# A four-layer cross-attention and mixture-of-experts kernel: three slots for the combine weights, three for the raw expert tiles, and several steps placed anew

## The chip, the cores and the metric

The kernel runs on one core of one Trainium2 chip, as one launch. The metric is the device time of that launch in microseconds (us), taken as the median of several runs. The core's engines are TensorE (PE; PEld is its weight load), VectorE (DVE), ScalarE (ACT), GpSimd (POOL) and SyncE (SP); SPq is SyncE's queue, from which most transfers are issued.

## The reference, cut to what matters

Tokens x are 4 x 256 rows of 256 numbers. Four layers follow one another; each adds a gated cross-attention against a context of 4 x 512 rows and then a gated feed-forward:

```python
x = x + tanh(g_xattn[i]) * xattn_i(layernorm(x), ctx)
x = x + tanh(g_ffn[i]) * ffn_i(layernorm(x))
```

Layers 0, 2 and 3 have attention with 16 heads of 16 numbers, layer 1 one with a single head (the "memory" attention). Feed-forwards 0, 1 and 3 are mixtures of experts: a router picks K of E experts per token (2 of 8, 2 of 8, 6 of 16), and a shared expert is added. Cut to its core, one of them is:

```python
probs = softmax(xf @ gate_w.T)
w, idx = top_k(probs, K)
combine = scatter(w, idx)                  # tokens x experts
act = silu(xf @ w_gate[e]) * (xf @ w_up[e])
out = sum_e(combine[:, e] * (act @ w_down[e])) + shared(xf)
```

Feed-forward 2 has no router: it multiplies by the signs of its weights, with 1024 hidden units.

## The kernel before, in words

**Precision.** Matrix operands in full precision are split in a high half (a rounded copy, written by ScalarE) and a low half (the difference, written by VectorE or GpSimd), and a product is the sum of three matmuls: high by high, high by low, low by high (`passes`, whose matmul is L615).

**Tiles of a feed-forward.** The hidden units of all experts stand one after another and are cut in tiles of 128: 14, 10, 8 and 25 tiles for the four feed-forwards. The tokens are cut in two halves of 512, and each half goes over all tiles, so feed-forward f has N = 2 x tiles steps: 28, 20, 16 and 50. For a tile n the work is:

- SyncE loads the raw weights in two pieces, gate and up (256 KB) and down (128 KB), in `load_tile` (L2039, issue at L2050), into one of RAWS = 4 slots; tiles 0 and 1 have places of their own. It loads the combine weights of this tile, one factor per hidden unit and token, as 256 KB from DRAM, in `load_weights` (L2074, issue at L2083), into one of 2 slots.
- ScalarE makes the high halves: `split_up` (L1883) and `split_down` (L1890). GpSimd makes the low ones: `lo_up` (L1931) and `lo_down` (L1936).
- TensorE: `gate(n)`, 6 matmuls of 512 columns, then `down(n-2)`, 12 of 256 columns, then `up(n)`, 6 of 512.
- ScalarE applies silu in place to the gate product (L1896). VectorE multiplies by the combine weights (`weighted`, L1970) and by the up product (`gated`, L1975). ScalarE takes the high half of the result (`half_hi`, L1872) and VectorE the low one (`half_lo`, L1985). `down(n)` multiplies these.

**Orders.** Each engine runs its instructions in the order in which they are written, and waits on counted semaphores. Per step n these orders are: ScalarE (L1916) split_up(n+1), half_hi(n-1), silu(n), split_down(n); GpSimd (L1955) lo_up(n+1), lo_down(n); VectorE (L2023) half_lo(n-1), weighted(n), gated(n); SyncE (L2095) load_tile(n+3), load_weights(n). The semaphores that matter here are f_w1r and f_w2r (counts of lo_up and lo_down done), f_w1h and f_w2h (of split_up and split_down), f_sw (of weighted done), f_hm (of gated), and d_fw (landings of combine weights). The waits on SyncE are:

```python
def load_tile(eng, n): ...       # for n >= 2 + RAWS, u piece then d piece
    w(eng, free, n - RAWS + 1)   # free: f_w1r for u, f_w2r for d (f_w1h, f_w2h in the third)
def load_weights(eng, n): ...
    w(eng, "f_sw", n - 1)
def sp(eng, first, last):
    for n in range(first, last + 1):
        if 2 + RAWS <= n + 3 < N:
            load_tile(eng, n + 3)
        if not sign:
            load_weights(eng, n)
```

`w(eng, kind, m)` waits until kind was counted m times within this feed-forward. The combine weights are first computed by the router (`route` on VectorE and ScalarE, `turn_weights` on TensorE, L1726 on ScalarE), written to DRAM by `weights_out` (L2065, L2069), and read back per tile. Combine weights of tiles 0 and 1 are loaded by `sp_weights` before the steps.

**Hooks, leads, followers.** Extra work is put between the steps of a feed-forward by the table HOOKS (L107): the last steps of the attention before ("late"), statistics, normalizing, turning and routing of the second half of the tokens, the addition to the tokens, the preparation of the memory attention ("mem"), and "extra" steps of GpSimd. LEADS (L128) puts the first keys and queries of the next attention into the feed-forward ahead of it, and SENDS (L140) says after which step SyncE sends those to DRAM. FOLLOW (L194) gives the places, within an attention's order (`order`, L233), of the statistics, turning and routing of the first half of the tokens of the feed-forward that comes next; its third number is that of the routing ("ro") and of what follows it. "au" copies constant rows into a keys buffer, "ms" is the root on GpSimd (L1111, L1114) for the normal form of keys or queries, "kk" the scaling by it (kn, L1291).

In the third feed-forward the "extra" step splits two weight matrices of layer 3, WQ and WO, on GpSimd (L2545, L2546). Before the second feed-forward, GpSimd clears the first queries buffer of layer 2 (`zero_stack`, L626).

Of the kernel before, what the change touches and what calls it, by code (L numbers as in the profile page):

```python
# [72 lines left out]
RAWS = 4  # L73
# [20 lines left out]
def hooks(first, *lists):  # L94
# [13 lines left out]
         4: [("late", "wn")], 5: [("statistics", 1), ("normal", 1)],  # L108
         6: [("turn", 1), ("halves", 1)], 8: [("logits", 1), ("route", 1, 0), ("route", 1, 1)],
# [6 lines left out]
         0: [("weights", 0), ("combine", 0), ("statistics", 1)], 1: [("normal", 1)],  # L116
# [4 lines left out]
         3: [("late", "wn")], 4: [("statistics", 1)], 5: [("normal", 1), ("extra", 0)],  # L121
         6: [("turn", 1), ("halves", 1)], 9: [("add", 0)]},
         {0: [("late", "ot"), ("late", "oe")], 1: [("late", "wo")], 2: [("late", "wd")],
         3: [("statistics", 1), ("normal", 1)], 4: [("turn", 1)], 5: [("halves", 1)],
         6: [("logits", 1)], 7: [("route", 1, 0)], 8: [("route", 1, 1)], 9: [("route", 1, 2)],
         10: [("weights", 1)], 12: [("combine", 1)], 26: [("add", 0)]}]
# [12 lines left out]

SENDS = {2: [("kw", 14), ("qw", 18)], 3: [("kw", 15), ("qw", 15)]}  # L140
# [53 lines left out]
FOLLOW = {0: (17.6, 4.6, 20), 2: (30.2, 9.2, 0), 3: (25.6, 9.2, 25.6)}  # L194
# [210 lines left out]
def flamingo(nc, a, out):  # L405
# [45 lines left out]
    ff_wl = at("ff_wl", PREG + (RAWS + 2) * BW * 4, [P, 2, 3 * D], F32R)  # L451
    pn = at("pn", KREG + 24576, [P, 2, M])
# [32 lines left out]
    for i in range(2):  # L485
# [5 lines left out]
            "s": at(f"ff_s{i}", q, [P, 2, HALF]), "w": at(f"ff_w{i}", q + 4096, [P, 2, HALF]),  # L491
# [77 lines left out]
    def before_attention(kind, blk):  # L569
        if (kind, blk) not in counted:  # L570
# [13 lines left out]
             ("d_small d_ident d_bias d_w2 d_w2n d_rows0 d_rows2 d_rows3 d_rows3a d_gate d_mask1 d_down d_fu0 d_fu1 d_fu2 d_fu3 d_fd0 d_fd1 d_fd2 d_fd3 d_fw0 d_fw1 d_wm "  # L584
# [971 lines left out]
    def counts(f, kind):  # L1556
# [173 lines left out]
    def feed_forward(f):  # L1730
# [231 lines left out]
        def dve(eng, heads=None, lead=None):  # L1962
# [554 lines left out]
    def _(eng):  # L2517
# [293 lines left out]
```

## Time and profile before

| | us |
|---|---|
| median of 3 runs | 1158.68 |
| lowest, highest | 1156.84, 1159.89 |
| the profiled execution's own time | 1151.56 |
| its span in the profile | 1149.8 |
| TensorE busy | 1009.6 (88%) |
| VectorE busy | 734.1 (64%) |
| ScalarE busy | 573.9 (50%) |
| GpSimd busy | 401.7 (35%) |

The profile is of one execution; its times run from the start of its span. Busy shares are means over stages of different kinds: the first attention runs to about 160 us, the first feed-forward to about 311, the memory attention to about 360, the second feed-forward to about 480, the second 16-head attention to about 640, the third feed-forward to about 705, the last attention to about 910, and the fourth feed-forward to the end. A wait is put down to the instruction whose semaphore came last. Matmuls overlap, so their durations add up to more than the time they take; the distance from one start to the next is what counts.

### The profile page before, as it was taken

Reading aid. Unit: us, or ns where it says so; the run is one execution under the profiler, and the core shown is the slowest. Engines: PE = TensorE matmul, PEld = TensorE weight load, DVE = VectorE, ACT = ScalarE, POOL = GpSimd, SP = SyncE. Lnnn points to the kernel's source line nnn. Section 1 sums busy time; section 2 is a strip of 40 time slices with the busy share of each in tenths; the row PEclk is TensorE's granted clock in tenths of the full one; section 3 lists DMA queues with packets and bytes.
Section 4 is the critical chain, followed back from the end, with each engine's and each line's share of the span. In section 5 each row is a group of like instructions: output and inputs, shape, how many; then the busy total and the mean of one; then the engine's idle time right before and its main releaser. Section 6 shows DMA issues by size and latency. Waiting matters only on the chain.

```text
span 1149.8 us, 18125 instructions
## 1 busy us (share of the span) xinstructions
PE 1009.6 (88%) x6456; PEld 766.3 (67%) x6456; DVE 734.1 (64%) x1639; ACT 573.9 (50%) x1129; POOL 401.7 (35%) x519
## 2 busy tenths in 40 slices
PE   4799868999877997789999866799999979999998
PEld 3566537878766876665664655566655568888887
DVE  6477757557767555688887755876676254545554
ACT  3688754445334543136667432265566535544443
POOL 5524413344204434523223024324210133444443
PEclk9899989899999998779999988899999989999999
DMA  6946624474320467754521345834521153555553
GB/s 180 244 94 149 137 62 148 128 195 134 115 99 7 135 160 178 135 87 122 131 48 40 106 111 97 149 92 76 129 44 32 17 159 115 153 158 162 159 156 108
DMA packets 82067, 136.54 MB, mean 119 GB/s; under 512 B 11565, under 2 KB 40518, under 8 KB 79546
## 3 DMA queue, kind: packets, MB, share of 16 engines
q1 hardware_dynamic: 71034, 101.93, 30.0%
q0 software_dynamic: 10944, 33.45, 17.1%
q8 instruction: 52, 0.85, 0.3%
q14 instruction: 37, 0.30, 0.1%
HBM read 113.41 MB, written 22.97 MB: 119 GB/s over the span
## 4 chain that ended last, share of the span: by engine, by line
PE 56%; DVE 17%; DMA 9%; ACT 6%; POOL 5%; issue 5%; SPq 1%; DVEq 0%; ACTq 0%; POOLq 0%
PE psum L615 34%; PE psum L908 7%; DMA ff_w<-weights_out 6%; PE psum L875 6%; PE psum L884 5%; ACT probs L1057 2%; DVE nmx L1373 1%; DVE nmx L1370 1%; DVE psum L1975 1%; POOL keys L1120 1%; PE psum L834 1%; DVE ff_s L1970 1%; DVE nmx L1371 1%; DMA weights_out<-combine 1%; DVE probs L1464 1%
## 5 line engine op out<-in xcount | busy, mean ns | idle before, releaser
L615 PE MATMUL psum<-ff_xh,ff_wh 128*128 128x512 f32 x424 | 176.3, 416 | 25.8 <-POOL ff_wl L1931 16.9
L1059 ACT ACTIVATE probs<-psum 128x512 f32<-128x512 f32 x256 | 144.1, 597 | 76.6 <-PE psum L875 73.0
L875 PE MATMUL psum<-queries,keys 128*128 128x512 f32 x384 | 154.9, 434 | 11.4 <-ACT probs L1057 5.9
L615 PE MATMUL psum<-ff_xh,ff_wl 128*128 128x512 f32 x392 | 156.4, 399 | 0.0
L1970 DVE TENSOR_TENSOR ff_s<-psum,ff_w 128x512 f32<-128x512 f32 x98 | 67.6, 689 | 126.3 <-DMA ff_w<-weights_out 116.5
L1931 POOL TENSOR_TENSOR ff_wl<-ff_raw,ff_wh 128x512 fp32r<-128x512 f32 x92 | 119.0, 1295 | 70.8 <-ACT ff_wh L1883 70.1
L1872 ACT ACTIVATE ff_hh<-psum 128x512 fp32r<-128x512 f32 x114 | 67.9, 596 | 143.0 <-DVE psum L1975 142.2
L615 PE MATMUL psum<-ff_wh,ff_hh 128*128 128x256 f32 x456 | 131.4, 292 | 4.8 <-DVE ff_hl L1985 4.6
L884 PE MATMUL psum<-keys,queries 128*128 128x512 f32 x256 | 117.1, 474 | 17.4 <-DVE nmx L1371 8.8
L615 PE MATMUL psum<-ff_wh,ff_hl 128*128 128x256 f32 x456 | 130.6, 290 | 0.0
L1936 POOL TENSOR_TENSOR ff_wl<-ff_raw,ff_wh 128x256 fp32r<-128x256 f32 x92 | 68.7, 746 | 172.1 <-ACT ff_wh L1890 172.1
L615 PE MATMUL psum<-ff_wl,ff_hh 128*128 128x256 f32 x392 | 113.4, 289 | 0.0
L615 PEld LDWEIGHTS psum<-ff_xh,ff_wh 128*128 128x128 f32 x424 | 83.5, 197 | 44.3 <-POOL ff_wl L1931 19.5
L908 PE MATMUL psum<-probs,values 128*32 128x256 f32 x1664 | 111.1, 390 | 2.2 <-DVE probs L1464 2.1
L1985 DVE TENSOR_TENSOR ff_hl<-psum,ff_hh 128x512 fp32r<-128x512 f32 x114 | 78.6, 689 | 47.7 <-ACT ff_hh L1872 46.8
L875 PEld LDWEIGHTS psum<-queries,keys 128*128 128x128 f32 x384 | 69.8, 191 | 52.8 <-ACT probs L1059 21.5
L615 PEld LDWEIGHTS psum<-ff_wh,ff_hh 128*128 128x128 f32 x456 | 91.1, 200 | 12.5 <-issue 7.8
L884 PEld LDWEIGHTS psum<-keys,queries 128*128 128x128 f32 x256 | 50.6, 200 | 63.5 <-DVE nmx L1371 25.3
L615 PEld LDWEIGHTS psum<-ff_wh,ff_hl 128*128 128x128 f32 x456 | 90.6, 199 | 0.7
L1057 ACT ACTIVATE probs<-psum,aug 128x512 f32<-128x512 f32 x128 | 80.3, 693 | 19.8 <-PE psum L875 19.7
L1373 DVE TENSOR_REDUCE nmx<-psum 128x1 f32<-128x512 f32 x128 | 80.8, 682 | 12.0 <-PE psum L884 11.4
L615 PEld LDWEIGHTS psum<-ff_xh,ff_wl 128*128 128x128 f32 x392 | 76.0, 194 | 17.2
(263 smaller groups left out, 2173.0 us busy)
## 6 DMA issues: line engine op xcount, KB each, us to landing
ff_w<-weights_out SPq DMA_DIRECT2D x94, 256.0 KB
ff_raw<-in_ff SPq DMA_DIRECT2D x92, 256.0 KB, 4.1
ff_raw<-in_ff SPq DMA_DIRECT2D x106, 128.0 KB, 2.2
keys_out<-keys_turned SPq DMA_DIRECT2D x24, 512.0 KB, 3.7
keys<-keys_out POOLq DMA_DIRECT2D x48, 256.0 KB, 5.0
queries_out<-queries_turned SPq DMA_DIRECT2D x24, 256.0 KB, 3.5
keys<-keys_out POOLq DMA_DIRECT2D x48, 128.0 KB, 5.4
queries<-queries_out POOLq DMA_DIRECT2D x32, 192.0 KB, 4.0
```

Of the source, the lines that this page charges most:

```text
L615: last = eng.matmul(dst, lhs[i](k), rhs[j](k), start=start and n == 0, stop=stop and n == groups * len(pairs) - 1, skip_group_check=True)
L875: then(eng.matmul(dst, kst[buf(c)][:, pair, kt * P:(kt + 1) * P], qst[buf(c)][:, :, pair, :], start=True, stop=True, skip_group_check=True ...
L884: then(eng.matmul(bank(st), qst[buf(b)][:, m, pair, qt * P:(qt + 1) * P], kst[buf(b)][:, pair, :], start=True, stop=True), "mx_full")
L908: last = eng.matmul(psum[32 * j:32 * j + 32, SUM_BANK, col:col + S], values[:, c % 2, slot, h * VW:h * VW + 32], probs[:, n % 3, i, j, :], ...
L1057: ins = eng.activation(dst, src, ACT.Exp, scale=SCALE, bias=aug0[:, KT * c + kt:KT * c + kt + 1])
L1059: ins = eng.activation(dst, src, ACT.Exp, scale=SCALE)
L1373: ins = eng.tensor_reduce(at_(0), bank(st), AX.X, ALU.max, negate=True)
L1872: then(eng.activation(ff_hh[:, slot, :], product(slot), ACT.Copy), "f_hh")
L1931: then(eng.tensor_tensor(ff_wl[:, slot, 0:2 * D], raw(n)[:, 0:2 * D], ff_wh[:, slot, 0:2 * D].bitcast(F32), ALU.subtract), "f_w1r")
L1936: then(eng.tensor_tensor(ff_wl[:, slot, 2 * D:3 * D], raw(n)[:, BD:BD + D], ff_wh[:, slot, BD:BD + D].bitcast(F32), ALU.subtract), "f_w2r")
L1970: then(eng.tensor_tensor(ff_s[:, slot, :], psum[:, GATE_BANKS[slot], :], ff_w[:, slot, :], ALU.mult), "f_sw")
L1985: then(eng.tensor_tensor(ff_hl[:, slot, :], product(slot), ff_hh[:, slot, :].bitcast(F32), ALU.subtract), "f_hr")
```

## The change

- The ring of raw expert tiles has three slots for four (RAWS), and the combine weights have three for two (WEIGHTS). The third one lies in the space of the fourth raw slot. The order of the loads on SyncE is as before.
- The places of hooks change: in the first and fourth feed-forwards normalizing, turning and the routing of the second half move by up to one step; in the third, the weight splits move from step 5 to step 9.
- The first keys and queries of the last attention, led in the third feed-forward, are placed anew, and both are sent after step 13 for 15.
- The routing of the first half is placed earlier in the first and last attention (20 to 13, 25.6 to 16).
- The clearing of the queries buffer moves from ahead of the second feed-forward to its hook 0 on GpSimd.

```diff
-RAWS = 4
+RAWS = 3
+
+WEIGHTS = 3
...
-         4: [("late", "wn")], 5: [("statistics", 1), ("normal", 1)],
-         6: [("turn", 1), ("halves", 1)], 8: [("logits", 1), ("route", 1, 0), ("route", 1, 1)],
+         4: [("late", "wn")], 5: [("statistics", 1)], 6: [("normal", 1)],
+         7: [("turn", 1), ("halves", 1)], 9: [("logits", 1), ("route", 1, 0), ("route", 1, 1)],
...
-         0: [("weights", 0), ("combine", 0), ("statistics", 1)], 1: [("normal", 1)],
+         0: [("weights", 0), ("combine", 0), ("extra", 0), ("statistics", 1)], 1: [("normal", 1)],
...
-         3: [("late", "wn")], 4: [("statistics", 1)], 5: [("normal", 1), ("extra", 0)],
-         6: [("turn", 1), ("halves", 1)], 9: [("add", 0)]},
+         3: [("late", "wn")], 4: [("statistics", 1)], 5: [("normal", 1)],
+         6: [("turn", 1), ("halves", 1)], 9: [("add", 0), ("extra", 0)]},
...
-         3: [("statistics", 1), ("normal", 1)], 4: [("turn", 1)], 5: [("halves", 1)],
-         6: [("logits", 1)], 7: [("route", 1, 0)], 8: [("route", 1, 1)], 9: [("route", 1, 2)],
-         10: [("weights", 1)], 12: [("combine", 1)], 26: [("add", 0)]}]
+         3: [("statistics", 1)], 4: [("normal", 1)], 5: [("turn", 1)], 6: [("halves", 1)],
+         7: [("logits", 1)], 8: [("route", 1, 0)], 9: [("route", 1, 1)], 10: [("route", 1, 2)],
+         11: [("weights", 1)], 13: [("combine", 1)], 26: [("add", 0)]}]
...
-         3: {7: [("au", 0), ("kp", 0, 0), ("sq", 0, 0), ("ms", 0, 0)],
-         8: [("kk", 0, 0), ("tk", 0, 0), ("te", 0, 0)],
-         10: [("kp", 0, 1), ("sq", 0, 1), ("ln", 0), ("ms", 0, 1), ("kk", 0, 1)],
-         11: [("tk", 0, 1), ("te", 0, 1), ("kw", 0), ("lm", 0)], 12: [("xt", 0), ("xe", 0)],
-         13: [("q", 0)], 14: [("sq", 0, 2), ("ms", 0, 2), ("kk", 0, 2), ("tq", 0), ("qe", 0)]}}
+         3: {7: [("kp", 0, 0), ("sq", 0, 0), ("ms", 0, 0)],
+         8: [("au", 0), ("kk", 0, 0), ("tk", 0, 0), ("te", 0, 0)],
+         10: [("kp", 0, 1), ("sq", 0, 1), ("ln", 0), ("ms", 0, 1), ("kk", 0, 1), ("lm", 0)],
+         11: [("xt", 0), ("xe", 0), ("tk", 0, 1), ("te", 0, 1), ("kw", 0)],
+         12: [("q", 0), ("sq", 0, 2), ("ms", 0, 2), ("kk", 0, 2)], 13: [("tq", 0), ("qe", 0)]}}
-SENDS = {2: [("kw", 14), ("qw", 18)], 3: [("kw", 15), ("qw", 15)]}
+SENDS = {2: [("kw", 14), ("qw", 18)], 3: [("kw", 13), ("qw", 13)]}
...
-FOLLOW = {0: (17.6, 4.6, 20), 2: (30.2, 9.2, 0), 3: (25.6, 9.2, 25.6)}
+FOLLOW = {0: (17.6, 4.6, 13), 2: (30.2, 9.2, 0), 3: (25.6, 9.2, 16)}
...
+    ff_w2 = at("ff_w2", PREG + (RAWS + 4) * BW * 4, [P, HALF])
...
             def weighted(n, slot):
-                eng.wait_ge(sems[f"d_fw{slot}"], (n // 2 + (ff_before(f, f"d_fw{slot}") + 1)) * 16)
+                s = n % WEIGHTS
+                eng.wait_ge(sems[f"d_fw{s}"], (n // WEIGHTS + (ff_before(f, f"d_fw{s}") + 1)) * 16)
                 w(eng, "f_sd", n + 1)
...
         def load_weights(eng, n):
-            slot, h = n % 2, half_of(n)
-            w(eng, "f_sw", n - 1)
+            slot, h = n % WEIGHTS, half_of(n)
+            w(eng, "f_sw", n - WEIGHTS + 1)
...
-        eng.wait_ge(sems["c_pv"], T)
-        zero_stack(eng, qst[FIRST_BUFFER[2]])
-        ff[1][2](eng, None, heads2)
+        def queries_cleared(_):
+            eng.wait_ge(sems["c_pv"], T)
+            zero_stack(eng, qst[FIRST_BUFFER[2]])
+
+        ff[1][2](eng, None, heads2, queries_cleared)
```

## Rows read from the trace of the kernel before

**Rows 1.** Page, part 4: the chain that ended last, by engine and by line.

```profile
PE 56%; DVE 17%; DMA 9%; ACT 6%; POOL 5%; issue 5%; SPq 1%; DVEq 0%; ACTq 0%; POOLq 0%
PE psum L615 34%; PE psum L908 7%; DMA ff_w<-weights_out 6%; PE psum L875 6%; PE psum L884 5%; ACT probs L1057 2%; DVE nmx L1373 1%; DVE nmx L1370 1%; DVE psum L1975 1%; POOL keys L1120 1%; PE psum L834 1%; DVE ff_s L1970 1%; DVE nmx L1371 1%; DMA weights_out<-combine 1%; DVE probs L1464 1%
```

**Rows 2.** Waits, whole span: who waited for whom, us, times, longest.

```profile
DVE ff_s L1970 <- DMA ff_w<-weights_out: 116.5, 67, 7.2
...
SPq L2050 <- POOL ff_wl L1936: 237.6, 76, 7.0
...
SPq L2083 <- DVE ff_s L1970: 38.6, 25, 10.6
```

**Rows 3.** Windows, fourth feed-forward: length, PE, PEld, DVE, ACT, POOL, PEclk, DMA, GB/s.

```profile
982.00:1130.00 148.00, 147.40 (x844) 129.31 (x843) 74.26 (x109) 72.05 (x142) 70.72 (x71) 1.00 0.54 158
```

**Rows 4.** Timeline, fourth feed-forward: start, length, engine, line, operation [idle before, releaser].

```profile
1003.23 0.69 DVE L1970 TENSOR_TENSOR ff_s<-psum,ff_w 128x512 f32<-128x512 f32 x1 [1.53 <-DMA ff_w<-weights_out]
...
1003.95 0.70 DVE L1975 TENSOR_TENSOR psum<-ff_s,psum 128x512 f32<-128x512 f32 x1
...
1004.68 0.60 ACT L1872 ACTIVATE ff_hh<-psum 128x512 fp32r<-128x512 f32 x1 [1.41 <-DVE psum L1975]
...
1005.17 0.59 ACT L1896 ACTIVATE psum<-psum 128x512 f32<-128x512 f32 x1
...
1005.69 0.40 ACT L1890 ACTIVATE ff_wh<-ff_raw 128x256 fp32r<-128x256 f32 x1
...
1006.17 0.74 POOL L1936 TENSOR_TENSOR ff_wl<-ff_raw,ff_wh 128x256 fp32r<-128x256 f32 x1 [1.53 <-ACT ff_wh L1890]
...
1007.31 0.60 SPq L2083 DMA_DIRECT2D ff_w<-weights_out  x1
...
1011.38 0.69 DVE L1970 TENSOR_TENSOR ff_s<-psum,ff_w 128x512 f32<-128x512 f32 x1 [1.54 <-DMA ff_w<-weights_out]
```

**Rows 5.** Page, part 6: DMA issues, count, KB each, median us to landing.

```profile
ff_raw<-in_ff SPq DMA_DIRECT2D x92, 256.0 KB, 4.1
ff_raw<-in_ff SPq DMA_DIRECT2D x106, 128.0 KB, 2.2
```

**Rows 6.** Chain in order of time, second feed-forward: start, us, what.

```profile
444.68 11.15 DMA ff_w<-weights_out
```

**Rows 7.** Timeline and tile ff_w: first and last weighted of the stretches.

```profile
176.02 0.68 DVE L1970 TENSOR_TENSOR ff_s<-psum,ff_w 128x512 f32<-128x512 f32 x1
...
293.43 0.69 DVE L1970 TENSOR_TENSOR ff_s<-psum,ff_w 128x512 f32<-128x512 f32 x1 [0.39 <-DMA ff_w<-weights_out]
...
368.28 0.69 DVE L1970 TENSOR_TENSOR ff_s<-psum,ff_w 128x512 f32<-128x512 f32 x1 [1.28 <-ACT psum L1896]
...
455.85 0.69 DVE L1970 TENSOR_TENSOR ff_s<-psum,ff_w 128x512 f32<-128x512 f32 x1 [7.16 <-DMA ff_w<-weights_out]
...
922.90 0.68 DVE L1970 TENSOR_TENSOR ff_s<-psum,ff_w 128x512 f32<-128x512 f32 x1
...
1130.24 0.69 DVE L1970 TENSOR_TENSOR ff_s<-psum,ff_w 128x512 f32<-128x512 f32 x1 [1.32 <-DMA ff_w<-weights_out]
...
L1970 DVE TENSOR_TENSOR ff_s<-psum,ff_w x98: 679/692/694, 174.7 to 1139.9; 128x512 f32<-128x512 f32 x98
```

**Rows 8.** Timeline of GpSimd, start of the second feed-forward.

```profile
356.82 3.51 POOL L626 MEMSET queries<- 128x4096 f32 x1 [9.94 <-PE psum L615]
...
374.25 0.74 POOL L1936 TENSOR_TENSOR ff_wl<-ff_raw,ff_wh 128x256 fp32r<-128x256 f32 x1 [2.47 <-ACT ff_wh L1890]
```

**Rows 9.** Timelines of ScalarE (fourth feed-forward's start) and VectorE (third feed-forward).

```profile
923.70 0.63 ACT L1883 ACTIVATE ff_wh<-ff_raw 128x512 fp32r<-128x512 f32 x1 [4.27 <-DMA ff_raw<-in_ff]
...
669.11 0.87 DVE L1291 SCALAR_TENSOR_TENSOR kn<-psum,rms,rows 128x256 f32<-128x256 f32 x2 [5.56 <-POOL rms L1114]
```

**Rows 10.** Timeline of TensorE, third feed-forward, at the lower clock.

```profile
698.09 0.63 PE L615 MATMUL psum<-ff_xh,ff_wh 128*128 128x512 f32 x1
698.52 0.63 PE L615 MATMUL psum<-ff_xl_second,ff_wh 128*128 128x512 f32 x1
```

More of the change, by code:

```diff
@@ L490, in flamingo @@
             "xl": [at(f"ff_xl{i}", k + 12288, [P, KC, HALF], F32R), xl_second],
-            "s": at(f"ff_s{i}", q, [P, 2, HALF]), "w": at(f"ff_w{i}", q + 4096, [P, 2, HALF]),
+            "s": at(f"ff_s{i}", q, [P, 2, HALF]), "w": [at(f"ff_w{i}{n}", q + 4096 + 2048 * n, [P, HALF]) for n in range(2)] + [ff_w2],
             "hh": at(f"ff_hh{i}", q + 8192, [P, 2, HALF], F32R),
@@ L583, in flamingo @@
              [f"d_w3{m}" for m in range(6)] +
-             ("d_small d_ident d_bias d_w2 d_w2n d_rows0 d_rows2 d_rows3 d_rows3a d_gate d_mask1 d_down d_fu0 d_fu1 d_fu2 d_fu3 d_fd0 d_fd1 d_fd2 d_fd3 d_fw0 d_fw1 d_wm "
+             ("d_small d_ident d_bias d_w2 d_w2n d_rows0 d_rows2 d_rows3 d_rows3a d_gate d_mask1 d_down d_fu0 d_fu1 d_fu2 d_fd0 d_fd1 d_fd2 d_fw0 d_fw1 d_fw2 d_wm "
               "d_cn0 d_cn1 d_out d_kw d_qw d_nw d_r00 d_r01 d_r10 d_r11 d_nr0 d_nr1 d_kept d_aq d_au0 d_au1").split())
@@ L1566, in counts @@
             return 2
-        if kind in ("f_d0", "f_d1", "f_d2", "f_d3"):
+        if kind in ("f_d0", "f_d1", "f_d2"):
             return len(range(int(kind[3]), n, RAWS))
@@ L1570, in counts @@
             return 0
-        if kind in ("d_fw0", "d_fw1"):
-            return TILES[f]
+        if kind in ("d_fw0", "d_fw1", "d_fw2"):
+            return len(range(int(kind[4]), n, WEIGHTS))
         return {"f_sd": n, "f_uf": n, "f_sw": n, "f_w1r": n, "f_w2r": n, "f_rt": 2, "f_re": 2,
@@ L1966, in weighted @@
             def weighted(n, slot):
-                eng.wait_ge(sems[f"d_fw{slot}"], (n // 2 + (ff_before(f, f"d_fw{slot}") + 1)) * 16)
+                s = n % WEIGHTS
+                eng.wait_ge(sems[f"d_fw{s}"], (n // WEIGHTS + (ff_before(f, f"d_fw{s}") + 1)) * 16)
                 w(eng, "f_sd", n + 1)
-                then(eng.tensor_tensor(ff_s[:, slot, :], psum[:, GATE_BANKS[slot], :], ff_w[:, slot, :], ALU.mult), "f_sw")
+                then(eng.tensor_tensor(ff_s[:, slot, :], psum[:, GATE_BANKS[slot], :], ff_w[s][:, :], ALU.mult), "f_sw")
             def gated(n, slot):
@@ L2074, in load_weights @@
         def load_weights(eng, n):
-            slot, h = n % 2, half_of(n)
-            w(eng, "f_sw", n - 1)
+            slot, h = n % WEIGHTS, half_of(n)
+            w(eng, "f_sw", n - WEIGHTS + 1)
             if n % tiles < ones:
-                eng.dma_start(ff_w[:, slot, :], a["one"].to_broadcast([P, HALF])).then_inc(sems[f"d_fw{slot}"], 16)
+                eng.dma_start(ff_w[slot][:, :], a["one"].to_broadcast([P, HALF])).then_inc(sems[f"d_fw{slot}"], 16)
                 return
@@ L2082, in load_weights @@
             src = wm[f][h][bass.ds(n % tiles, 1), :, :].rearrange("one g (r c) -> (one g) r c", r=1)
-            eng.dma_start(ff_w[:, slot, :], src.to_broadcast([RUNS, RUN, HALF])).then_inc(sems[f"d_fw{slot}"], 16)
+            eng.dma_start(ff_w[slot][:, :], src.to_broadcast([RUNS, RUN, HALF])).then_inc(sems[f"d_fw{slot}"], 16)
         def sp_weights(eng):
```

## The prediction

> **What bounds the kernel now.** I begin with the chain of work that ended last [rows 1]: over half is TensorE, a third its expert products, and 6% of the span is the landing of combine weights (ff_w, one 256 KB transfer per tile). The chain cannot say why they land late, so next come the waits. VectorE waits 116.5 us for ff_w in 67 places; SyncE, which issues these transfers, waits 237.6 us for GpSimd's L1936 (the low half of a tile's down part, lo_down) and 38.6 us for VectorE's use of ff_w [rows 2]. So most combine loads go out late because SyncE stands in front of a raw-tile load, not because their slot is full. Third, the fourth feed-forward away from its edges: TensorE is busy 147.4 of 148 us at full granted clock [rows 3]. There the wait for ff_w is covered; only just, as one tile shows.
>
> [rows 4] is that tile in order of time, W(n) being the start of L1970 for tile n (weighted). With n = 16: W(16) 1003.23, L1975 (gated), L1872 at 1004.68 (half_hi 16), then in ScalarE's written order silu(17) 1005.17, split_down(17) 1005.69, GpSimd's lo_down(17) 1006.17 to 1006.91. SyncE waited for that; it issues the down piece of tile 21, and at 1007.31 w(18), which lands at 1011.38, when W(18) starts. Through the transfer, this circle is 4.08 us up to the issue and 4.07 us to the landing, **8.15 us**, and before the change it carries **two** tiles (W(16) to W(18)): 4.08 us per tile, a hair under TensorE's 4.2 (35 tiles in the stretch of rows 3).
>
> **The change, part by part.**
>
> *Three raw slots.* Step n of sp() first loads tile n+3, which waits until tile n+3-RAWS is split; only then load_weights(n). With four slots that was lo_down(n-1); with three it is lo_down(n). load_weights itself is relaxed (f_sw >= n-2 for n-1), but it still stands behind, and nothing in the diff moves it. So w(n) is issued after lo_down(n), which follows silu(n) and half_hi(n-1) on ScalarE, which follow gated(n-1) and W(n-1). The same circle of 8.15 us now carries **one** tile: W(n) = W(n-1) + 8.15. Every link has its row in [rows 4], down piece and up piece still go out beside w as now, so I take 4.07 us for the landing: the same transfer in the same company. Bounds for it: the 128 KB piece alone, 2.2 us [rows 5], and 11.15 us, w(16) of the second feed-forward beside the key transfers [rows 6].
>
> It holds for the tiles with n+3 < N: n = 2 to 24 in the first, 2 to 16 in the second, 2 to 46 in the fourth, 23 + 15 + 45 = 83. The third has no combine weights. From [rows 7], W(1) to the last such tile:
> first: 23 x 8.15 = 187.5 against 293.43 - 176.02 = 117.4, +70.0;
> second: 15 x 8.15 = 122.3 against 455.85 - 368.28 = 87.6, +34.7;
> fourth: 45 x 8.15 = 366.8 against 1130.24 - 922.90 = 207.3, +159.4.
> Together +264.1 us. TensorE's 4.2 us fit inside 8.15, and so do the hooks on VectorE (three instructions of 0.7 us per tile leave it 6 us).
>
> *Ends.* The last three loads wait for no raw tile: W(46) to W(49) is 9.7 us now [rows 7]; with TensorE caught up it is three times W to the end of the next silu (1005.17 + 0.59 - 1003.23, some 2.6), 7.7. Taken as -2 in each of three, -6.
>
> *Second feed-forward, first loop.* lo_down(2) ended at 374.99 [rows 8]; plus 0.40 and 4.07 it gives W(2) at 379.5, 11.2 after W(1) where I counted 8.15: +3.0. Around its hook 14 the keys go out and in and w(16) took 11.15 instead of 4.07 [rows 6]; inside the longer loop some of these 7.1 us are covered: 0 to 7.1, taken +4.
>
> *Clearing.* The 3.51 us memset of the queries stands on GpSimd before lo_up(0) of the second feed-forward [rows 8]; behind lo_down(1) it has slack, as lo_up(2) waits for its tile. lo_up(0), which gate(0) waits for, starts when the high half is there; the router's products cover part. Between 0 and -3.5: -1.7, half.
>
> *Routing earlier in the attention (FOLLOW).* Same instructions, other places. In the fourth, weights_out and w(0), w(1) stand on SyncE before tiles 2 to 4, and ScalarE waited 4.27 us for tile 2 [rows 9]; with the combine ready sooner those loads go when the attention's probs are free: -4.3. Bounds 0 and -4.3, as only that wait goes. In the first feed-forward no such wait shows: 0.
>
> *Weight splits WQ, WO from hook 5 to 9 of the third feed-forward.* Now GpSimd waits for those matrices and splits them ahead of the root of the first keys; VectorE's kn waited 5.56 us for it [rows 9]. Moved behind it, with the constant rows, that goes: -5.6. They come before the next keys' root, which VectorE asks for later. Late next is the queries' round trip; keys and queries sent two tiles sooner are taken at 0, bound -3 to +3. Its three raw slots: a tile's pieces land in 2.2 us and are asked for two tiles ahead, 0. Statistics and roots apart, logits a hook later: VectorE and GpSimd idle in the loop, 0; without it, each would cost its own duration.
>
> Sum: 264.1 - 6 + 3.0 + 4 - 1.7 - 4.3 - 5.6 = +253.5. The profiled execution took 1151.56 us (span 1149.8), so 1405. The median of the runs, 1158.68, lies 7.1 above it; I add that: **1412**.
>
> By the page "DMA: Bandwidth & Descriptors" of the Trainium skill, section "Anatomy of one DMA", a GpSimd-path transfer takes 2.0 us plus its bytes at 436 GB/s, 2.6 us for 256 KB. An estimate by that page puts the circle at 6.7 us and the time at 1290; the trace's 4.07 us disagrees, and the sum goes by the trace.
>
> **The rivals.**
>
> *B, the same loop with a quicker landing.* Half the bytes per microsecond could mean an emptier queue. For: w shares its queue with 384 KB of raw pieces now. Against: these are issued just before and after w in both kernels, so its company is the same. Price at a landing midway between 2.2 and 4.1 us [rows 5], 3.2: circle 7.3, 83 x 0.9 = -75: 1337.
>
> *C, the clock falls and TensorE matters.* It idles about 4 us per tile, in one piece mostly. At the lower level (1.2 GHz) matmuls of 512 columns start 0.43 us apart [rows 10]; 12 of these and 12 of half the columns make some 7.7 us per tile, against 4.2 now. That still fits in 8.15, but hooks with transposes or an attention's late steps no longer do: 0.4 us per tile, +33: 1445. Against: the products lie beside the circle, not in it.
> The Trainium skill, "TensorE: Matmul & The Clock Gate", Part 1, says the array drops to half clock when idle and recovers only under sustained activity. By that page alone C's lower clock is to be expected; its price hangs on the rows.
>
> *D, faster.* If the raw-tile wait did not gate w(n), that is if its slot were what ends last, three slots would lift the ff_w landings out of the chain: 6% of 1149.8, 69 us, and the 11.6 us of starts above (1.7 + 4.3 + 5.6): 1158.7 - 81 = 1078. It decides from the point where SyncE's wait before L2050 is over by the time the slot is free. Against: 237.6 us to 38.6 [rows 2]; and w(18) went out 0.40 us after lo_down(17).
>
> *E, no change*: the circle lies beside the end anyway. It would need 8.15 us to hide behind 4.2; nothing does that.
>
> **How the numbers follow.** Forecast 0.73, B 0.13, C 0.11, D 0.02, E 0.01. The likeliest gives 1412. The range reaches from B to past C, and holds a circle of 7.2 to 8.7 us (83 x -0.95 and +0.55): 1335 to 1460. A difference under about 0.3% cannot be told from none by a measurement here. Slower 0.97, same 0.01, faster 0.02.
>
> **What would show it.** Right: in the fourth feed-forward L1970 follows L1970 by about 8.15 us; before each, w is issued 4 us earlier and 0.4 us after that same tile's L1936; TensorE is busy half the time; the ff_w landings become the largest part of the chain; VectorE waits for ff_w some 5 us per tile, over 350 us. B shows as L2083 to L1970 near 3.2 us, C as matmuls 0.43 us apart and a period beyond 8.3. In the third, kn no longer waits 5 us. I am wrong if w(n) is issued before lo_down(n): then a period near 4.2 stays and D holds.

## The result, and the profile after

The changed kernel takes **1463.91 us** (median of 4 runs, 1459.24 to 1470.76), against 1157.76 for the kernel before, run beside it (4 runs, 1154.86 to 1159.89). The ratio is 1.267 [1.2625, 1.2715], +306 us. Forecast were 1412 and a range up to 1460, so the time lies 4 us outside it. The profiled execution took 1470.76 us, its span 1468.9, with a mean granted clock of 0.901 of full speed (before 0.95).

Of the changed kernel's page, parts 1 and 4 and the rows of part 6 that answer to [rows 1, 5]:

```profile
PE 1105.8 (75%) x6456; PEld 812.1 (55%) x6456; DVE 727.8 (50%) x1639; ACT 563.7 (38%) x1129; POOL 398.3 (27%) x519
...
PE 30%; DMA 26%; DVE 20%; ACT 9%; POOL 7%; issue 6%; SPq 2%; ACTq 0%; DVEq 0%; POOLq 0%
DMA ff_w<-weights_out 23%; PE psum L618 13%; PE psum L911 5%; PE psum L878 4%; POOL ff_wl L1939 4%; PE psum L887 4%; DVE psum L1979 4%; DVE ff_s L1974 4%; ACT psum L1899 3%; SPq L2054 2%; ACT ff_wh L1893 2%; ACT probs L1060 1%; DVE nmx L1376 1%; DMA keys<-keys_out 1%; DVE nmx L1373 1%
...
ff_raw<-in_ff SPq DMA_DIRECT2D x92, 256.0 KB, 4.0
ff_raw<-in_ff SPq DMA_DIRECT2D x106, 128.0 KB, 2.1
```

The landing of the combine weights went from 6% of the span to 23% (69 to 338 us). Behind it stand the other members of the circle, one line each: lo_down (L1939), gated (L1979), weighted (L1974), silu (L1899), split_down (L1893). TensorE's expert products fell from 34% to 13%. The rows of part 6 are what they were, so the raw loads are as quick as before.

The waits of the changed kernel (us, times, longest), the first three and SyncE's row that answers to [rows 2]:

```profile
ACT ff_hh L1875 <- DVE psum L1979: 538.7, 92, 16.3
POOL ff_wl L1939 <- ACT ff_wh L1893: 488.7, 85, 11.1
DVE ff_s L1974 <- DMA ff_w<-weights_out: 464.3, 81, 15.4
...
SPq L2054 <- POOL ff_wl L1939: 578.7, 83, 13.5
```

Four engines wait for each other in a ring, each 5.7 to 7.0 us at a time. SyncE stands in front of a raw load for lo_down 83 times: the 23 + 15 + 45 tiles that the prediction counted.

One tile in the stretch that has no hooks, in order of time, as in [rows 4] (the changed kernel's timeline, fourth feed-forward; SPq L2087 issues the combine load):

```profile
1259.60 0.69 DVE L1974 TENSOR_TENSOR ff_s<-psum,ff_w 128x512 f32<-128x512 f32 x1 [5.39 <-DMA ff_w<-weights_out]
...
1261.05 0.60 ACT L1875 ACTIVATE ff_hh<-psum 128x512 fp32r<-128x512 f32 x1 [6.24 <-DVE psum L1979]
1261.54 0.59 ACT L1899 ACTIVATE psum<-psum 128x512 f32<-128x512 f32 x1
1262.06 0.40 ACT L1893 ACTIVATE ff_wh<-ff_raw 128x256 fp32r<-128x256 f32 x1
...
1262.54 0.74 POOL L1939 TENSOR_TENSOR ff_wl<-ff_raw,ff_wh 128x256 fp32r<-128x256 f32 x1 [6.19 <-ACT ff_wh L1893]
...
1263.68 0.60 SPq L2087 DMA_DIRECT2D ff_w<-weights_out  x1
...
1267.70 0.69 DVE L1974 TENSOR_TENSOR ff_s<-psum,ff_w 128x512 f32<-128x512 f32 x1 [5.33 <-DMA ff_w<-weights_out]
```

1259.60 to 1263.68 is 4.08 us to the issue, the same as before; 4.02 to the landing; 8.10 us in all, and now one tile for each turn. The next one took 8.56 (landing 4.41). From W(11) at 1159.41 to W(46) at 1450.66 it is 291.25 / 35 = 8.32 us a tile. Of that the part up to the issue is 4.09 in the mean, within 0.02 of 4.08 in 33 of the 35 tiles; the landing is 4.23 in the mean and varies from 3.65 to 5.00.

TensorE in that stretch, which answers to [rows 3] (columns as there), and its first matmul of the tile above:

```profile
1160.00:1450.00 290.00, 185.31 (x840) 142.94 (x840) 73.65 (x109) 68.05 (x141) 69.38 (x70) 0.91 0.27 80
```

```profile
1260.43 0.47 PE L618 MATMUL psum<-ff_xh,ff_wh 128*128 128x512 f32 x1 [3.03 <-DVE ff_s L1974]
```

Busy 64% of the stretch where it was 99.6%, and idle 3 us in every tile. DMA share and GB/s have halved too, so it is not bandwidth that is short.

The mean granted clock of 0.91 covers two kinds of tiles: in 20 of the 35 it is 1.00, in the other 15 it lies between 0.59 and 0.81. The very next tile is one of these. Soon after its idle 2.96 us the matmuls have the spacing of the lower level, 0.43 us [rows 10]:

```profile
1268.54 0.47 PE L618 MATMUL psum<-ff_xh,ff_wh 128*128 128x512 f32 x1 [2.96 <-DVE ff_s L1974]
...
1269.16 0.63 PE L618 MATMUL psum<-ff_xh,ff_wl 128*128 128x512 f32 x1
1269.59 0.63 PE L618 MATMUL psum<-ff_xh,ff_wh 128*128 128x512 f32 x1
```

The part up to the issue is 4.09 us in the tiles at full clock and 4.10 in the others, so in this stretch the clock stays outside the circle.

### The profile page after: what moved, and what is told of

Read it like the earlier page. It is cut to its first block, busy times and chain, and to the rows that moved or that the text cites. A ratio compares the mean times of both kernels' runs of the same rounds, so it can differ in the third digit from the quotient of the medians.

```text
span 1468.9 us, 18126 instructions
## 1 busy us (share of the span) xinstructions
PE 1105.8 (75%) x6456; PEld 812.1 (55%) x6456; DVE 727.8 (50%) x1639; ACT 563.7 (38%) x1129; POOL 398.3 (27%) x519
## 4 chain that ended last, share of the span: by engine, by line
PE 30%; DMA 26%; DVE 20%; ACT 9%; POOL 7%; issue 6%; SPq 2%; ACTq 0%; DVEq 0%; POOLq 0%
DMA ff_w<-weights_out 23%; PE psum L618 13%; PE psum L911 5%; PE psum L878 4%; POOL ff_wl L1939 4%; PE psum L887 4%; DVE psum L1979 4%; DVE ff_s L1974 4%; ACT psum L1899 3%; SPq L2054 2%; ACT ff_wh L1893 2%; ACT probs L1060 1%; DVE nmx L1376 1%; DMA keys<-keys_out 1%; DVE nmx L1373 1%
## 5 line engine op out<-in xcount | busy, mean ns | idle before, releaser
L618 PE MATMUL psum<-ff_xh,ff_wh 128*128 128x512 f32 x424 | 193.1, 455 | 185.3 <-DVE ff_s L1974 131.4
L1974 DVE TENSOR_TENSOR ff_s<-psum,ff_w 128x512 f32<-128x512 f32 x98 | 67.6, 690 | 474.7 <-DMA ff_w<-weights_out 464.3
L1939 POOL TENSOR_TENSOR ff_wl<-ff_raw,ff_wh 128x256 fp32r<-128x256 f32 x92 | 68.0, 739 | 488.7 <-ACT ff_wh L1893 488.7
L618 PE MATMUL psum<-ff_wh,ff_hh 128*128 128x256 f32 x456 | 146.9, 326 | 33.6 <-DVE ff_hl L1989 31.3
L618 PE MATMUL psum<-ff_xh,ff_wl 128*128 128x512 f32 x392 | 170.9, 436 | 0.0
L618 PE MATMUL psum<-ff_wh,ff_hl 128*128 128x256 f32 x456 | 140.2, 311 | 0.0
L618 PEld LDWEIGHTS psum<-ff_wh,ff_hh 128*128 128x128 f32 x456 | 103.6, 227 | 61.2 <-issue 51.8
L887 PE MATMUL psum<-keys,queries 128*128 128x512 f32 x256 | 117.3, 474 | 17.6 <-DVE nmx L1374 8.1
L618 PE MATMUL psum<-ff_wl,ff_hh 128*128 128x256 f32 x392 | 124.2, 317 | 0.0
L618 PEld LDWEIGHTS psum<-ff_wh,ff_hl 128*128 128x128 f32 x456 | 101.5, 223 | 0.6
L618 PE MATMUL psum<-ff_xl,ff_wh 128*128 128x512 f32 x212 | 93.4, 440 | 0.0
L618 PEld LDWEIGHTS psum<-ff_wl,ff_hh 128*128 128x128 f32 x392 | 90.0, 230 | 2.8
L618 PE MATMUL psum<-ff_xl_second,ff_wh 128*128 128x512 f32 x212 | 90.8, 428 | 0.0
```

Source lines behind the costliest of these rows:

```text
L618: last = eng.matmul(dst, lhs[i](k), rhs[j](k), start=start and n == 0, stop=stop and n == groups * len(pairs) - 1, skip_group_check=True)
L887: then(eng.matmul(bank(st), qst[buf(b)][:, m, pair, qt * P:(qt + 1) * P], kst[buf(b)][:, pair, :], start=True, stop=True), "mx_full")
L1939: then(eng.tensor_tensor(ff_wl[:, slot, 2 * D:3 * D], raw(n)[:, BD:BD + D], ff_wh[:, slot, BD:BD + D].bitcast(F32), ALU.subtract), "f_w2r")
```

## The experiments

Theory T, throughout: with three raw slots the load that stands ahead of the combine load in SyncE's order ties w(n) to lo_down(n), and a circle of some 8.2 us carries one tile. The rivals: the smaller ring of raw slots costs by itself; the placements cost; TensorE's clock costs; the landing is slower with three slots. Expectations are quoted as they were recorded; a ratio is that to the kernel before on the same chip, with its 95% interval. The kernels did not all run on the same chip, so a difference of a few microseconds between two of them is judged by whether their intervals overlap.

**1. The combine load first.** The changed kernel, with two calls exchanged:

```diff
 def sp(eng, first, last):
     for n in range(first, last + 1):
+        if not sign:
+            load_weights(eng, n)
         if 2 + RAWS <= n + 3 < N:
             load_tile(eng, n + 3)
-        if not sign:
-            load_weights(eng, n)
...
```

> The changed kernel with one edit: at each step SyncE issues the combine load of tile n ahead of the raw load of tile n+3, so w(n) stands behind lo_down(n-1) and no longer behind lo_down(n). Theory one (a circle of 8.3 us that carries one tile): the circle carries two tiles again, the time falls from 1464 to 1130 to 1165 us, and in the fourth feed-forward the distance between two starts of weighted falls from 8.35 to about 4.2 us. Rival (the placements of hooks or the smaller raw ring make it slow): little changes, 1430 us or more.

1148.09 us (10 runs, 1140.50 to 1153.14), ratio 0.994 [0.9913, 0.9968]. Exchanging two calls takes 316 us off the changed kernel, with its three raw slots and every placement kept. So neither ring size nor placements cost 300 us. Its timeline, fourth feed-forward:

```profile
1015.29 0.74 POOL L1939 TENSOR_TENSOR ff_wl<-ff_raw,ff_wh 128x256 fp32r<-128x256 f32 x1 [1.29 <-ACT ff_wh L1893]
1016.06 0.33 SPq L2054 DMA_DIRECT2D ff_raw<-in_ff  x1
1016.43 0.60 SPq L2087 DMA_DIRECT2D ff_w<-weights_out  x1
1016.75 0.69 DVE L1974 TENSOR_TENSOR ff_s<-psum,ff_w 128x512 f32<-128x512 f32 x1 [1.62 <-DMA ff_w<-weights_out]
...
1019.69 0.73 POOL L1939 TENSOR_TENSOR ff_wl<-ff_raw,ff_wh 128x256 fp32r<-128x256 f32 x1 [1.51 <-ACT ff_wh L1893]
1020.07 0.69 DVE L1974 TENSOR_TENSOR ff_s<-psum,ff_w 128x512 f32<-128x512 f32 x1 [0.54 <-DMA ff_w<-weights_out]
```

The load issued at 1016.43 is used at 1020.07. It goes out after the lo_down of the tile before (1015.29) and 3.3 us ahead of its own tile's (1019.69): two tiles to a circle again, median period 4.35 us in the fourth feed-forward.

**2. Slots alone, and 3. placements alone.** The kernel before with `RAWS = 3` and `WEIGHTS = 3` and nothing else; the changed kernel with `RAWS = 4`, `WEIGHTS = 2` and its placements.

> The kernel before with only the slots changed (three raw, three combine); hooks, leads, sends, routing and clearing stay as before. Theory one: all of the loss is here, 1455 to 1490 us, as the placements were worth some -10 us. Rival (placements make the loss): near 1160 us.

> The changed kernel with four raw slots and two combine slots again: only the placements are left of the change. Theory one, with the terms of the prediction (-1.7, -4.3 and -5.6 us, and a first feed-forward that starts 5 us later in the changed trace): 1145 to 1158 us. Rival (placements make the loss): over 1300 us.

Slots alone: 1476.68 (4 runs), ratio 1.2774 [1.2702, 1.2846]. Placements alone: 1140.05 (4 runs), 0.9869 [0.9824, 0.9915]. The slots cost 322 us by themselves, as expected. The placements gain 15 us without the slots, 5 us beyond the expected range (my terms for them came to 11.6). Beside the slots they gain some 13 (1476.68 against 1463.91), but there the intervals overlap.

**4. Two combine slots** in the changed kernel (`WEIGHTS = 2`, three raw slots):

> The changed kernel with two combine slots for three, still three raw ones. Theory one: the wait on the combine slot is never the last one, so the third slot is worth nothing, 1455 to 1472 us, no difference from the changed kernel. Rival (the third slot gives something that the raw ring takes away): slower than the changed kernel by over 15 us, one landing less ahead in the last three tiles of each stretch.

1463.89 (4 runs), 1.2663 [1.2608, 1.2718]: the changed kernel's time to 0.02 us. As the order of the loads stands, the third combine slot is worth nothing; the loss is the fourth raw slot's absence alone.

**5. The company of the landing.** The down piece is issued behind the combine load, the wait kept ahead of it:

```diff
 if 2 + RAWS <= n + 3 < N:
-    load_tile(eng, n + 3)
+    load_tile(eng, n + 3, "u")
+    w(eng, "f_w2h" if sign else "f_w2r", n + 1)
 if not sign:
     load_weights(eng, n)
+if 2 + RAWS <= n + 3 < N:
+    load_tile(eng, n + 3, "d")
```

> The changed kernel, but in each step the down piece of tile n+3 is issued behind w(n) instead of ahead of it; w(n) still waits for lo_down(n). It measures the company of the combine load inside an unchanged circle: 0.38 us of SyncE's issue time goes, and if the 128 KB piece ahead of it cost landing time, that too. Theory one (circle of 8.35 us, landing 4.2): 0.4 to 1.2 us less per tile, 83 times, so 1365 to 1430 us. Rival (the landing has a fixed length whatever is ahead): only the 0.38 us, 1432 us.

1419.63 (2 runs), 1.2299 [1.2257, 1.2342]: 44 us less than the changed kernel, 0.53 per tile of 83; the median period in the fourth feed-forward is 7.72. The issue of the down piece took 0.38 of the circle; the rest, some 0.15 us, would be what a 128 KB piece ahead of it adds to the landing. Its size is uncertain: over the 83 tiles the landing is 4.10 us in the mean here, 4.38 in the changed kernel and 4.26 in kernel 4, which has the changed kernel's order of loads. What is left is 4.1 us, so the piece ahead is not what makes the distance to the 2.1 us of a 128 KB transfer. The size is the nearer explanation: raw pieces of 256 KB land in 4.1 us before and 4.0 after, pieces of 128 KB in 2.2 and 2.1 [rows 5].

**6. split_down earlier.** On ScalarE it goes ahead of half_hi(n-1) and silu(n), which cuts the link from gated(n-1) to lo_down(n):

```diff
 if n < N - 1:
     split_up(n + 1, 1 - slot)
+if not sign:
+    split_down(n, slot)
 half_hi(n - 1, 1 - slot)
 if not sign:
     silu(n, slot)
-split_down(n, slot)
...
```

> The changed kernel with one link of the circle cut on ScalarE: split_down(n) stands ahead of half_hi(n-1) and silu(n), so it no longer waits for weighted(n-1). SyncE's order is untouched. Theory one: the circle then closes only through down(n) on TensorE and carries two tiles in about 10.1 us (0.4 + 4.2 landing, 2.8 to half_lo, 1.4 down, 1.3 for the two splits), 5.0 us per tile: 1170 to 1230 us. Rival (SyncE's wait for the raw tile or TensorE's falling clock is what costs, not this link): over 1400 us.

1273.20 (2 runs), 1.1031 [1.0995, 1.1066]. The order of the loads is untouched and 191 us are gone, so that link is in the circle. The size I had wrong (1170 to 1230 expected): tiles without hooks alternate between about 4.2 and 6.4 us, those with hooks take 9 to 13.6. What bounds the long ones wasn't followed further.

**7 and 8. A delay of one instruction in the circle.** A ScalarE copy of 128x512 ahead of half_hi, 0.5 us from start to start, into the space of the third combine slot. In 7 it is put into kernel 4 (a circle of one tile), in 8 into kernel 1 with two combine slots (a circle of two):

```diff
+if not sign and n > 2:
+    eng.activation(spare[:, :], product(slot), ACT.Copy)
 # half_hi's own activation, unchanged
...
```

> The kernel of r4 with one more ScalarE copy of 128x512 ahead of each half_hi, into the space of the third combine slot: 0.5 us (start to start) added to the circle. Theory one: the circle carries one tile and nothing hides it, +0.5 us 83 times, some +42 us: 1495 to 1515 us. Rival (something else bounds the tile, such as TensorE at its lower clock): under +15 us.

> The same added 0.5 us ScalarE copy as in r7, but in the kernel of r1 (combine load first, so the circle carries two tiles); two combine slots. Theory one: the circle is lengthened from 8.35 to 8.85 us for two tiles, 4.42 per tile where TensorE needs 4.2, so at most 0.25 us for 83 tiles: 1150 to 1172 us, a third or less of the 42 us expected in r7. Rival (ScalarE's added work costs what it lasts wherever it stands): 1148 + 42 = 1190 us.

7: 1492.31 (2 runs), 1.2929 [1.2890, 1.2968], +28 us against kernel 4. 8: 1160.24 (10 runs), 1.0034 [1.0012, 1.0056], +12 us against kernel 1. In the quiet stretch of the fourth feed-forward (tiles 12 to 46) the part up to the issue grew by the whole delay, from 4.09 to 4.58 us in the mean. Two tiles of it (VectorE's weighted, here L1976, and the copy, L1876, in front of half_hi):

```profile
1201.78 0.69 DVE L1976 TENSOR_TENSOR ff_s<-psum,ff_w 128x512 f32<-128x512 f32 x1 [5.10 <-DMA ff_w<-weights_out]
...
1203.24 0.60 ACT L1876 ACTIVATE spare<-psum 128x512 f32<-128x512 f32 x1 [5.95 <-DVE psum L1981]
1203.73 0.59 ACT L1877 ACTIVATE ff_hh<-psum 128x512 fp32r<-128x512 f32 x1
...
1210.42 0.69 DVE L1976 TENSOR_TENSOR ff_s<-psum,ff_w 128x512 f32<-128x512 f32 x1 [5.37 <-DMA ff_w<-weights_out]
```

I had expected 83 x 0.5 = 42. But the edit delays half_hi(3) and later ones only, which are the circles of 21 + 13 + 43 = 77 tiles, 38 us. In the traces the issues come 29.9 us later in all: the copy adds 0.5 to nearly every tile, and nothing where GpSimd's root, the keys or TensorE already holds the circle up (tiles 4, 6 and 20 of the first feed-forward are such); in the two logits' tiles named further on the issue even comes 1.5 and 1.8 us earlier. With two tiles to a circle it costs less than half of that. Kernel 8 differs from kernel 1 by the third combine slot too, so the 12 us are the price of both, and how they divide was not run. The recorded rival, by which ScalarE's added work costs what it lasts wherever it stands, called for 1190 us; 1160.24 rules it out.

**9. Placements with four raw slots, combine load first** (kernel 3 with the edit of kernel 1):

> Four raw slots, two combine slots, the placements of the change, and the combine load ahead of the raw load at each step. Theory one: the circle closes through the slot alone (weighted(n-2) to w(n) to weighted(n), some 5.4 us for two tiles) and TensorE's 4.2 us per tile bound the quiet stretches; where hooks made the old circle late it gains: 1105 to 1138 us against 1140 for r3. Rival (the raw tiles now land late behind the combine loads): no gain or a loss against r3.

1121.52 (4 runs), 0.9723 [0.9687, 0.9759]. Windows and waits of it, for [rows 3, 2]:

```profile
970.00:1090.00 120.00, 120.00 (x692) 106.01 (x691) 59.32 (x91) 62.69 (x115) 58.51 (x58) 1.00 0.54 160
```

```profile
DVE ff_s L1973 <- DMA ff_w<-weights_out: 22.0, 9, 6.4
```

VectorE's wait for combine weights falls from 116.5 us (118.0 in kernel 3) to 22.0 and TensorE has not one idle hundredth in 120 us. The exchange is worth 18.5 us even to a ring of four (1140.05 to 1121.52; 17 by the ratios): the wait of [rows 2] was not all covered.

**10 and 12. The hooks apart.** In 10 (from the changed kernel), GpSimd takes the root and ScalarE the exponentials one hook later than now, so that the result for which each waits is there; the routing steps in the first feed-forward move one hook on. 12 is the same in kernel 9.

```diff
-"route": lambda e, h, p: part.exponentials(e, h, B1) if p == 0 else None,
+"route": lambda e, h, p: part.exponentials(e, h, B1) if p == 1 else None,
...
-does = {"statistics": lambda e, h: part.root(e, h), "extra": lambda e, i: extra(i),
+does = {"normal": lambda e, h: part.root(e, h), "extra": lambda e, i: extra(i),
```

> The changed kernel; GpSimd's root and ScalarE's exponentials for the second half of the tokens are done one hook after the VectorE step that feeds them, and in the first feed-forward the routing parts 1 and 2 one hook later. Theory one (these hooks tie work behind weighted(n) on VectorE to lo_down(n+1) or half_hi(n) on the others and so lengthen the circle): in the fourth feed-forward the tile after the statistics falls from 10.9 to about 8.4 us and the one with the exponentials from 11.0 to about 9.8; in all 6 to 12 us less than the changed kernel, 1452 to 1458 us. Rival (the long tiles come from transfers or the clock): no change of these two tiles.

> The kernel of r9 (1121.5 us) with the hooks apart as in r10. Theory one: with the circle off the path these hooks have slack, 1112 to 1124 us. Rival (the hooks delay TensorE's tiles there too): over 5 us less than r9.

10: 1459.26 (5 runs), 1.2640 [1.2615, 1.2664]. That is 4.6 us less than the changed kernel, with overlapping intervals, and just short of the range expected. In the fourth feed-forward the root's tile went from 10.91 us to 8.10 and the exponentials' from 10.97 to 8.37, but their new tile takes 9.85 and one of 13.85 appeared in the first feed-forward; the logits' tile stayed at 10.72. Summed over the 83 tiles, the parts up to the issue are 1.9 us shorter than in the changed kernel: moving the hooks took 12.6 us out of five tiles and put nearly as much into others. So the hooks are shown to lengthen their tiles, and this way of moving them is not shown to gain. 12: 1126.04 (4 runs), 0.9752 [0.9727, 0.9777], above the range expected, a miss. It is 4.5 us more than kernel 9, within the intervals: with two tiles to a circle moving these hooks gained nothing.

**11. The combine load one step ahead**, in the changed kernel: w(n+1) at step n, ahead of the raw load (three tiles to a circle, the third slot used):

```diff
-if 2 + RAWS <= n + 3 < N:
-    load_tile(eng, n + 3)
-if not sign:
-    load_weights(eng, n)
+if not sign and n == 2:
+    load_weights(eng, 2)
+if not sign and n + 1 < N:
+    load_weights(eng, n + 1)
+if 2 + RAWS <= n + 3 < N:
+    load_tile(eng, n + 3)
...
```

> The changed kernel (three raw, three combine slots) with the combine load of tile n+1 issued at step n, ahead of the raw load: then the third slot is used. Theory one: w(n+1) stands behind lo_down(n-1) and weighted(n-2), the circle carries three tiles and is off the path; the quiet stretches are bound by TensorE at 4.2 us: 1110 to 1140 us, at or below r1 (1148) and near r9 (1121). Rival (three raw slots are too few in any order): no better than r1.

1126.15 (4 runs, 1124.90 to 1128.05), 0.9757 [0.9735, 0.9780]. VectorE's wait for ff_w is 17.1 us in 6 places. It is 22 us quicker than kernel 1, with which it shares everything but the step at which w is issued. It writes into the third slot while two are in use; what it would be with two was not run.

**13. The first routing late.** Kernel 9 with the third number of FOLLOW[0] back at 20:

> The kernel of r9 with one number set back: the routing of the first feed-forward's first half stands at 20 again instead of 13 in the first attention's order. Theory: the earlier place makes ScalarE wait 2.65 us for VectorE's routing step in the middle of the softmax, and the first feed-forward's second weighted start at 180 to 182 us where it was 176.0 (and 175.4 in r2, which has the old places); so 4 to 6 us come back and the time is 1114 to 1118 us, against 1121.5 for r9. Rival (the later start comes from another placement): it stays at 180 us or more, and 1119 to 1124 us.

1118.42 (6 runs, 1114.80 to 1118.91), 0.9684 [0.9646, 0.9721], the lowest median of all. It is 3.1 us below kernel 9, with overlapping intervals, and 0.4 above the range expected. W(1) of the first feed-forward starts at 178.46 for 180.03, so it went only part of the way back to 176.02. Four raw and three combine slots at once were not tried: the third combine slot lies in the space of the fourth raw one.

## Why the prediction was right in kind and 52 us short

**What held.** The order of waits, the count of 83 and the circle of one tile are in the trace, and kernels 1, 4, 6, 7 and 8 show them by experiment. From W(1) to the last tile of each ringed stretch the changed kernel takes 203.5, 148.6 and 383.2 us, 735.2 in all, where 412.3 were. The gain around the third feed-forward held too: from the end of the second to W(1) of the fourth it is 441.2 us for 450.6, -9.3 where -9.9 was forecast, and VectorE's 5.56 us wait for the root and ScalarE's 4.27 us wait for tile 2 are gone.

**Where the 66 us lie** (the spans differ by 319.1, the forecast was +253.5):

*The landing, mis-sized.* I took 4.07 us from one tile of [rows 4]; over 11 tiles before the mean was 4.16, and after it is 4.23. The period is 8.32 for 8.15: 83 x 0.17 = **14 us**.

*Hook tiles, the step that failed.* "Statistics and roots apart, logits a hook later: VectorE and GpSimd idle in the loop, 0" was wrong. 83 x 8.32 and the 7 us forecast for the second feed-forward make 697.6; measured 735.2. Nearly all of these **38 us** sit in tiles with hooks. The idle time I counted as cover is not free: an engine idle 6 us per tile is idle because it is waiting for the circle, and a step that stands ahead of its link in the written order and waits for something of the same turn is in the circle. Taken tile by tile, the part from W(n-1) to the issue of w(n) is longer than 4.09 us by:

| what holds up lo_down | tiles | us |
|---|---|---|
| a root on GpSimd | five, 1.6 to 2.7 each | 11.0 |
| exponentials on ScalarE, with a table load | three, 2.3 to 2.4 each | 7.2 |
| logits: split_down waits for TensorE | two, 1.9 and 2.7 | 4.5 |
| the keys, on GpSimd | one | 3.2 |
| not followed: tile 2 of the first and fourth feed-forward | two, 1.2 each | 2.4 |

Two landings of the second feed-forward are longer than 4.23 by 6.7 (the keys' tile) and 4.7 (tile 9, 8.92 us; the combine weights of the second half are written out right behind its issue, and that this is the cause was not tested). Together 39.7, of which 4 were forecast; some 2 us are spread over the rest. The changed kernel, root tile (W(3) 1085.01, W(4) 1095.92, 10.91 us):

```profile
1088.19 0.17 DVE L1618 TENSOR_SCALAR ve<-mv 128x4 f32<-128x4 f32 x1
...
1088.44 1.03 POOL L1609 TENSOR_TENSOR rstd<-ve,half_neg 128x4 f32<-128x4 f32 x1 [8.00 <-DVE ve L1618]
1089.46 1.25 POOL L1934 TENSOR_TENSOR ff_wl<-ff_raw,ff_wh 128x512 fp32r<-128x512 f32 x1
1090.68 0.72 POOL L1939 TENSOR_TENSOR ff_wl<-ff_raw,ff_wh 128x256 fp32r<-128x256 f32 x1
```

GpSimd stood in the root, waiting for a VectorE step that is written behind W(3), with lo_up and lo_down behind it. lo_down came 2.7 us late, and so did the combine load. Nor is the price the root's own 1.03 us, as my "without it, each would cost its own duration" had it: what counts is when the result that it waits for comes. The exponentials' tile (W(8) 1131.66, W(9) 1142.63, 10.97 us) is the same on ScalarE, ahead of half_hi and silu, with a table load for Silu after it:

```profile
1133.50 0.26 ACT L1678 ACTIVATE rt_w<-rt_w 128x64 f32<-128x64 f32 x1 [5.70 <-DVE rt_w L1694]
1134.18 0.58 ACT L1875 ACTIVATE ff_hh<-psum 128x512 fp32r<-128x512 f32 x1
1134.77 1.28 ACT L1899 ACT_TABLE_LOAD   x1
```

Kernel 10 moved just these, and their tiles fell by 2.8 and 2.6 us. Its loops are 10.3 us shorter in all, but 8.4 of that is in the landings, and kernel 4's, whose hooks are the changed kernel's, are shorter by as much (10.1). The logits' tile (10.70 us) looks like rival C: its matmuls start 0.43 us apart, as in [rows 10], and silu and split_down wait for TensorE there.

```profile
1121.71 0.63 PE L618 MATMUL psum<-ff_xh,ff_wl 128*128 128x512 f32 x1
...
1123.66 0.58 ACT L1899 ACTIVATE psum<-psum 128x512 f32<-128x512 f32 x1 [0.64 <-PE psum L618]
...
1126.08 0.42 ACT L1893 ACTIVATE ff_wh<-ff_raw 128x256 fp32r<-128x256 f32 x1 [1.84 <-PE psum L618]
```

Tile 4 of the second feed-forward (10.58 us) is the same kind. That is read from the traces and wasn't tried by itself.

*The keys, mis-sized*, inside those 38. I took +4 for the key round trip in the second feed-forward. The tile is 18.2 us (W(14) 584.91, W(15) 603.11), 9.9 over a plain one, 6 more than forecast. GpSimd waits 7.85 us for the outgoing keys ahead of lo_up and lo_down, so the issue comes 3.2 us late, and the load, issued beside the incoming keys, lands 10.9 us after it.

```profile
587.76 2.03 POOL L1123 DMA_DIRECT2D keys<-keys_out  x4 [7.85 <-DMA keys_out<-keys_turned]
591.70 1.98 POOL L1123 DMA_DIRECT2D keys<-keys_out  x4
592.18 0.59 SPq L2087 DMA_DIRECT2D ff_w<-weights_out  x1
...
603.11 0.69 DVE L1974 TENSOR_TENSOR ff_s<-psum,ff_w 128x512 f32<-128x512 f32 x1 [15.42 <-DMA ff_w<-weights_out]
```

The cover I subtracted is not there: what waits for the landing is the circle itself. In the traces of kernels 2, 4, 7 and 10 this tile takes 16.0 to 16.9 us, so 1 to 2 us of the 18.2 are of this one execution.

*Outside the loops*: -3.8 for a forecast -17.6, **14 us**. The first feed-forward's W(1) comes at 181.33 for 176.02, +5.3 where I had 0 for the earlier routing. It is the placements' doing: slots alone start at 175.39, placements alone at 182.09. Kernel 13 puts the routing back and recovers 1.6 us in its trace (178.46, where W(1) of the other kernels with the early routing lies between 179.8 and 182.3) and 3.1 in the median, which the intervals do not bear out. The rest, some 2.5 us, is not settled. What the trace shows of the early routing is that ScalarE now stops in the middle of an attention's softmax for VectorE:

```profile
149.17 0.18 ACT L1677 ACTIVATE rt_c<-psum 128x4 f32<-128x4 f32 x1 [2.66 <-DVE rt_w L1694]
```

The other 8 us: the three ends came to +1.3, -1.3 and -1.6 for -2 each, the stretch from the first feed-forward's last tile to the second's W(1) is 1.5 us longer where the clearing was to give -1.7, and the gain of 9.3 named above was 0.6 short. (Why the clearing gave nothing was not looked into.)

14 + 38 + 14 is 66. The profiled run lies 6.8 us above its median where I had added 7.1 to mine, which is why the medians are 52 apart and not 66. That the miss looks 14 us smaller by the medians is the luck of which executions were profiled.

**The rivals.** B (a quicker landing): none; 4.2 us with half the bytes per microsecond. D (faster): no, kernel 4 shows the third slot worth 0 while the raw load stands ahead of it; but part of the 69 us that D named was real time: by the order of the issues, kernels 9 and 11 stand 18.5 and 14 us below kernel 3. C as I priced it (+33) did not come, though the lower level did. After the gap ahead of 1260.43 matmuls start 0.31 and then 0.23 us apart, after the next 0.43; 15 of the 35 quiet tiles have a stretch at the lower level, and the root's tile has a mean granted clock of 0.69. The only tiles found in which TensorE holds up split_down, and so the circle, are the two with the logits, 4.5 us together.

By the Trainium skill, "TensorE: Matmul & The Clock Gate", Part 1, an idle array drops to half clock; the trace agrees only in part, as TensorE idles some 3 us in every quiet tile and 20 of the 35 kept a granted clock of 1.00 all the same.
By its page "DMA: Bandwidth & Descriptors", "Anatomy of one DMA", 256 KB take 2.6 us on the GpSimd path; measured on SyncE's queue are 4.02 and 4.41 here, and the 1290 us worked out from it was further off than the sum by rows.

## What to carry to other kernels

A queue that issues in written order turns a wait for one buffer into a wait for all that stands behind it: before a ring is made smaller, look at what is issued behind its load, and put what is needed soonest first. The number of slots says nothing by itself; the time is the length of the circle divided by the tiles that it carries, and one call exchanged with the next changed that number from one to two (1463.9 to 1148.1 us). Once a circle bounds, an idle engine is not cover by itself: whatever stands ahead of its link and makes that link start later costs that delay, as five roots of 0.7 to 1.0 us cost 11.0 us here. So hooks priced at 0 under the old bound must be priced again, each by when the result that it waits for is there.

## What the runs showed that I had not expected

The exchange of the two calls is worth some 18 us with four raw slots too, and with the first routing put back the kernel stands at 1118.42, 3.2% below the one before. With three raw slots, the load put one step ahead (kernel 11) comes within 5 us of kernel 9 with its four. The landing of a 256 KB combine load stayed near 4.2 us when the traffic around it fell from 158 to 80 GB/s. And cutting the circle on ScalarE (kernel 6) gave tiles of two lengths in turn, 4.2 and 6.4 us, rather than one of the mean. Up to the issue the circle hardly varies: summed over the 83 tiles, the parts from W(n-1) to the issue come to 371.4 us in the changed kernel and in kernel 4 alike, while the landings come to 363.8 and 353.8; what scatters between executions is the landing.
